# Two expert ids read straight from memory, a reordered head, and low parts moved to GpSimd, in an AdaLN-style MoE and FFN kernel

## What is computed

```python
# each batch b has an expert id e = itok_B_0_7[b] and a language id itok_B_0_3[b]
h = relu(x @ (wi.T + 2*common_i + 2*expert_i[e]))       # 128 -> 512, both corrections of rank 16
c = h @ (wo.T + 2*common_o + 2*expert_o[e])             # 512 -> 128
cur = c
for r in range(4):                                      # four rounds of a mixture of four experts
    logits = cur @ Wg[r] + bg[r]
    w = softmax(top2(logits))                           # weight per expert and token
    cur = cur + sum_e w[e] * (gelu(cur @ W1[e] + b1[e]) @ W2[e] + b2[e])
x = x + cur
z = x @ lora_A[lang] @ lora_B[lang] + lang_embed[lang]  # in the kernel a product with a merged 128x128 matrix
y = silu((z @ w1) * s1) * ((z @ w2) * s2)
y = gelu(gelu(y @ h1 * t1) @ h2 * t2)
x = x + (y @ w3) * s3
```

## Time and profile before

| | us |
|---|---|
| median of three runs | 485.16 |
| the three runs | 484.31, 485.16, 489.13 |
| profiled execution, its whole time | 486.61 |
| its span, first to last instruction | 484.8 |
| TensorE busy in the span | 477.9 |
| VectorE busy | 387.7 |
| ScalarE busy | 393.9 |
| GpSimd busy | 118.7 |

### The profile page before, as it was taken

How to read it: one execution, slowest core, us unless ns; L and a number is a source line. 1 busy time by engine, 2 the same in 40 slices (tenths; PEclk the granted TensorE clock), 3 DMA queues, 4 the chain that set the end, 5 groups by cost and what they waited for, 6 DMA issues and landing times.

```text
span 484.8 us, 7478 instructions
## 1 busy us (share of the span) xinstructions
PE 477.9 (99%) x2270; PEld 397.0 (82%) x2270; DVE 387.7 (80%) x641; ACT 393.9 (81%) x542; POOL 118.7 (24%) x102
## 2 busy tenths in 40 slices
PE   7999999999999999999999999999999999999997
PEld 7998888888888888888888888888888887888885
DVE  4789899999879898988898898889897758554343
ACT  3799988888888888988888888888888888697653
POOL 5796212121212112121222121231313144400000
PEclk9999999999999999999999999999999999999999
DMA  7702702020201102020202012120202000000001
GB/s 209 215 5 88 266 18 89 2 87 3 87 11 76 71 16 87 0 87 0 87 0 87 11 76 82 49 89 0 87 2 87 2 0 0 1 0 1 0 22 69
DMA packets 6986, 26.30 MB, mean 54 GB/s; under 512 B 2226, under 2 KB 2610, under 8 KB 4786
## 3 DMA queue, kind: packets, MB, share of 16 engines
q1 hardware_dynamic: 5826, 21.20, 12.1%
q0 software_dynamic: 528, 3.67, 2.2%
q10 hardware_dynamic: 608, 1.11, 0.8%
HBM read 24.81 MB, written 1.18 MB: 54 GB/s over the span
## 4 chain that ended last, share of the span: by engine, by line
PE 96%; DMA 2%; SPq 1%; issue 0%; DVE 0%
PE bank L505 34%; PE bank L506 34%; PE bank L509 26%; DMA stage<-lora_all 2%; PE bank L594 1%; PE bank L595 1%; PE bank L527 1%; SPq L244 0%; SPq L247 0%; PE bank L540 0%; PE bank L524 0%; SPq L257 0%; DVE x L1276 0%; SPq L345 0%; SPq L344 0%
## 5 line engine op out<-in xcount | busy, mean ns | idle before, releaser
L812 ACT ACTIVATE act_out<-bank,vec 128x512 f32<-128x512 f32 x256 | 165.4, 682 | 41.8 <-PE bank L509 32.6
L1115 DVE TENSOR_TENSOR hid_lo<-act_out,hid_hi 128x1024 fp32r<-128x1024 f32 x128 | 156.6, 1243 | 33.3 <-ACT hid_hi L817 33.2
L817 ACT ACTIVATE hid_hi<-act_out 128x1024 fp32r<-128x1024 f32 x128 | 135.9, 1062 | 8.0 <-PE bank L509 0.2
L468 POOL TENSOR_TENSOR cur<-cur,prod 128x512 f32<-128x512 f32 x48 | 64.9, 1352 | 238.4 <-DVE prod L1126 237.9
L505 PE MATMUL bank<-hid_hi,moe_hi 128*128 128x512 f32 x256 | 99.9, 390 | 0.0
L509 PE MATMUL bank<-hid_hi,moe_lo 128*128 128x512 f32 x256 | 99.7, 390 | 0.0
L505 PE MATMUL bank<-xhi,moe_hi 128*128 128x512 f32 x256 | 99.7, 390 | 0.0
L506 PE MATMUL bank<-hid_lo,moe_hi 128*128 128x512 f32 x256 | 99.7, 389 | 0.0
L506 PE MATMUL bank<-xlo,moe_hi 128*128 128x512 f32 x256 | 99.6, 389 | 0.0
L509 PE MATMUL bank<-xhi,moe_lo 128*128 128x512 f32 x256 | 99.6, 389 | 0.0
L505 PEld LDWEIGHTS bank<-hid_hi,moe_hi 128*128 128x128 f32 x256 | 48.1, 188 | 11.3 <-issue 0.2
(11 more groups left out here) (126 smaller groups left out, 569.9 us busy)
## 6 DMA issues: line engine op xcount, KB each, us to landing
cw_all<-cw_dram SPq DMA_DIRECT2D x16, 1024.0 KB, 4.6
stage<-ffn_w POOLq DMA_DIRECT2D x1, 2304.0 KB, 8.5
cw_all<-moe_w SPq DMA_DIRECT2D x4, 512.0 KB, 10.3
stage<-lora_all SPq DMA_DIRECT2D x5, 160.0 KB, 7.1
x<-x_t POOLq DMA_DIRECT2D x3, 256.0 KB, 7.0
out_t<-x SPq DMA_DIRECT2D x3, 256.0 KB, 2.5
cur<-cond_base ACTq DMA_DIRECT2D x2, 256.0 KB, 3.1
stage<-ffn_w POOLq DMA_DIRECT2D x1, 512.0 KB, 3.8
```

Source lines behind the costliest of these rows:

```text
L468: pool.tensor_tensor(cur[:, c, :], cur[:, c, :], prod[:, s % 2, :], ALU.add).then_inc(add_done, 1)
L812: act.activation(act_out[:, f // 2, f % 2, :], bank[:, f, :], ACT.Gelu_apprx_tanh, bias=vec[:, V_B1 + e * FC + f:V_B1 + e * FC + f + 1]).t ...
L817: act.activation(hid_hi[:, s % 2, 2 * pr:2 * pr + 2, :], act_out[:, pr, :, :], ACT.Copy)\
L1115: dve.tensor_tensor(hid_lo[:, s % 2, 2 * pr:2 * pr + 2, :], act_out[:, pr, :, :], hid_hi[:, s % 2, 2 * pr:2 * pr + 2, :].bitcast(F32), ALU ...
```

## The change

- **Ids.** The expert ids of batches 0 and 1 are read into registers straight from batch_ids in memory, on SyncE and on ScalarE. The SBUF copy ids is still loaded, behind SyncE's first factor load, for the others.
- **Loads.** ScalarE issues x(0) between the two factor loads of batch 1 and not ahead of them, and lora 3 behind the cast x0_high(0). x(1) to x(3) move from GpSimd's queue to SyncE's, between and behind the lora loads.
- **TensorE.** WARM is 7 and not 13; two more warm-ups stand between the first two merge groups. cond_hidden(0) stands ahead of merge groups 2 and 3, cond_out(1) ahead of group 5, cond_out(2) ahead of group 6, and a few calls near the end of the head change places; expert_in(0, 0, 0, (3,)) now stands ahead of merge_lang.
- **GpSimd.** It takes over split_gate, x0_low(2) and the low parts of the conditioned chunks 3 and 2, which it makes from cur and not from PSUM, behind the last moe_low. Its memsets of prod stand behind them.
- **Orders.** SUMS, HIGHS, LOWS, MERGE_BANKS and the lists of VectorE and ScalarE are adapted.

```diff
-MERGE_BANKS = (6, 7, 4, 5, 2, 3, 6, 7, 5, 6, 7, 5, 6, 7, 5, 6)
+MERGE_BANKS = (6, 7, 4, 5, 6, 7, 4, 5, 5, 6, 7, 5, 6, 7, 5, 6)
...
-WARM, KEEP_WARM = 13, 2
+WARM, KEEP_WARM = 7, 2
...
+        def first_expert(queue, b):
+
+            return queue.value_load(batch_ids[0:1, b:b + 1], min_val=0, max_val=LORA_EXPERTS - 1)
+
+        def first_load(queue, b, kind, e):
+            arrived = (lora_in, first_out_in)[kind][b]
+            queue.dma_start(lora[lora_rows(b, kind), 0, :],
+                            lora_all[bass.ds(e, 1), 2 * RANK * kind:2 * RANK * (kind + 1), :]
+                            .rearrange("e r n -> (e r) n")).then_inc(arrived, 16)
...
         @block.sync
         def _(sp):
+            first = first_expert(sp, 0)
+            first_load(sp, 0, 0, first)
             sp.dma_start(ids[:], batch_ids).then_inc(ids_in, 16)
+            first_load(sp, 0, 1, first)
             sp.dma_start(vec[:], vecs).then_inc(small_in, 16)
             sp.dma_start(gbias[:], gate_bias.to_broadcast([SQ, ROUNDS * EXPERTS])).then_inc(small_in, 16)
             sp.wait_ge(ids_in, 16)
-            first_load(sp, 0)
-            expert = lora_expert(sp, 2)
-            sp.wait_ge(base_in[0], 16)
-            expert_load(sp, 2, expert)
-            for b in (4, 5, 6, 7):
+            for b in (2, 4, 5):
                 lora_load(sp, b)
+            x_load(sp, 1)
+            for b in (6, 7):
+                lora_load(sp, b)
+            x_load(sp, 2)
+            x_load(sp, 3)
...
-            pool.wait_ge(first_out_in[1], 16)
-            for c in range(1, CHUNKS):
-                x_load(pool, c)
...
+            def conditioned_low(c):
+                pool.wait_ge(cond_cur, c + 1)
+                pool.tensor_tensor(xlo[:, c, :], cur[:, c, :], xhi[:, c, :].bitcast(F32), ALU.subtract)\
+                    .then_inc(xs_done, 1)
...
             moe_low(6)
             moe_low(3)
             moe_low(7)
+            conditioned_low(3)
+            conditioned_low(2)
...
-            pool.wait_ge(xs_done, CHUNKS)
+            pool.wait_ge(cond_cur, CHUNKS)
             for i in range(2):
                 pool.memset(prod[:, i, 0:1], 0.0).then_inc(add_done, 1)
...
+                elif b == PER_CHUNK * (CHUNKS - 1):
+                    pe.wait_ge(cond_cur, c)
                 elif b % PER_CHUNK == 0:
                     pe.wait_ge(xs_done, c)
...
             merge_group(0)
+            warm(KEEP_WARM)
             merge_group(1)
             warm(KEEP_WARM)
+            cond_hidden(0)
             merge_group(2)
             merge_group(3)
-            cond_hidden(0)
             cond_hidden(1)
             merge_group(4)
             cond_out(0)
             cond_hidden(2)
+            cond_out(1)
             merge_group(5)
-            cond_out(1)
...
             cond_out(6)
+            cond_out(7)
             expert_in(0, 0, 0, (2,))
-            cond_out(7)
+            expert_in(0, 0, 0, (3,))
             merge_lang()
-            expert_in(0, 0, 0, (3,))
...
             base_load(act, 0)
-            x_load(act, 0)
             act.wait_ge(const_done, 1)
             act.activation(low_any[0:1, :], blank[0:1, 0:1], ACT.Gelu_apprx_tanh)
+            second = first_expert(act, 1)
+            first_load(act, 1, 0, second)
+            x_load(act, 0)
+            first_load(act, 1, 1, second)
+            base_load(act, 1)
+            x0_high(0)
             act.wait_ge(ids_in, 16)
-            first_load(act, 1)
-            base_load(act, 1)
             lora_load(act, 3)
-            x0_high(0)
             merged_high(0, 0)
             merged_high(1, 0)
...
-            first_gelu(2)
-            moe_high(7)
-            first_high(0)
-            conditioned_high(3)
+            first_gelu(2)
+            first_gelu(3)
             conditioned_copy(3)
```

More of the change, by code:

```diff
@@ L685, in _ @@
             cond_hidden(2)
+            cond_out(1)
             merge_group(5)
-            cond_out(1)
             cond_hidden(3)
             cond_hidden(4)
+            cond_out(2)
             merge_group(6)
-            cond_out(2)
             cond_out(3)
@@ L695, in _ @@
             cond_hidden(6)
+            first_logits(1)
             cond_out(4)
             cond_out(5)
-            first_logits(1)
             cond_hidden(7)
@@ L939, in _ @@
             relu_high(7)
-            first_gelu(0)
             moe_high(6)
             tanh_gate(0)
+            moe_high(3)
+            first_gelu(0)
+            moe_high(7)
             first_gelu(1)
-            moe_high(3)
+            conditioned_high(3)
+            first_high(0)
             first_gelu(2)
-            moe_high(7)
-            first_high(0)
-            conditioned_high(3)
+            first_gelu(3)
             conditioned_copy(3)
+            first_high(1)
             lang_high(0)
-            first_gelu(3)
             lang_high(1)
-            first_high(1)
             with act.Fori(0, ROUNDS - 1) as rnd:
@@ L1245, in _ @@
             gate_choice(0, 0)
-            conditioned_low(2)
             gate_gap(0, 0)
             relu_low(7)
+            gate_weights(0, 0, True)
             gate_logits(1, 0)
-            gate_weights(0, 0, True)
             gate_order(1, 0)
+            hidden_low(0, 0, (0,))
             gate_choice(1, 0)
             gate_gap(1, 0)
-            hidden_low(0, 0, (0,))
-            conditioned_low(3)
             hidden_low(0, 0, (1,))
```

127 lines of the change are left out of this document (59 added, 68 removed).

## The result

The changed kernel takes 496.75 us (median of 6 runs, 495.84 to 497.24). The kernel before took 485.27 beside it (6 runs, 484.31 to 489.13). The ratio is 1.0234, 95% interval 1.0215 to 1.0253: slower by 11.5 us. The forecast was 486.3 us with a range to 488.5. It was wrong by 10.5 us, and on the wrong side of one per cent.

What follows compares the result with a forecast made beforehand. Prediction: TensorE bounds the kernel (busy 477.9 of 484.8 us). Head +0.2 us and wait for GpSimd's two lows +0.95 sum to +1.15 on the median 485.16, giving 486.3 us; range 482.8 to 488.5.

## What to carry to other kernels

Work moved to a slack engine is paid for from when that engine gets there, so follow the mover's whole list back to its last wait, and put a signal that another engine waits for ahead of work that nobody needs yet: here a swap of two calls is worth 5.2 us, and the memsets ahead of the lows 5.8. Size a stop of TensorE with what its clock does behind it, and don't take out warm-ups because they stand in a wait. Compare heads only with an execution whose time is the median's. And check a granted clock of 1.00 against the spacing of the matmuls before you believe it.

## What the runs showed that was not expected

- A subtraction of 128x512 on GpSimd takes 1.28 to 1.30 us, and 2.25 to 2.29 beside VectorE's subtraction with both inputs in SBUF, which itself took 2.13 and not 1.20.
- A stop of 4.8 us brought the clock to 1.2 GHz for the next 4.6 us of work; stops of 1.57 and 1.38 us at the same place did not. In the head, waits of 1.15 and 1.44 us with 1.8 us of work between them did (0.50 from 8 to 14 us in the run with the ids from SBUF).
- The granted clock read 1.00 in the head of after while the matmuls of cond_hidden(0) stood 0.213 us apart, the spacing that goes with 0.51 in the kernel before.
- A pointer load took 0.86, 1.10 and, beside the transfer of x on the same queue, 1.70 us.
- The head of one kernel moved by 2.4 us from one execution to the other (merge_group(4) of before at 15.90 and at 13.53), with the landing of the factors (waits of 1.78 and 0.81 us) and the clock behind it.
